# A five-pass graph network on one core: run masks, edge weights and factors put into PSUM, and the relation tiles laid over fewer PSUM banks

## The chip, the cores and the metric

The kernel runs on one core of a Trainium2 chip. Its engines are TensorE (PE, matrix products), VectorE (DVE), ScalarE (ACT), GpSimd (POOL) and SyncE (SP), each with its own instruction stream; they meet through semaphores alone. SBUF is the large on-chip memory, PSUM is a small one of eight banks of 512 fp32 words in each of 128 partitions, which the matrix products write. The metric is the time of one execution on the device in microseconds.

## The reference

Four graph layers run one after the other over 12500 nodes with 16 channels and 400000 edges, which come sorted by target node. Each layer gathers a node's row for each edge, makes a message of it, and sums the messages over the edges of a target; a residual and a normalisation follow.

```python
weights = (relu(edge_attr @ W1 + b1) @ W2 + b2).reshape(-1, 16, 16)   # layer 0
out = segment_sum(einsum('ei,eio->eo', x[src], weights), dst) + x @ root
msg = xw[r] * (dis[r] * ew * dis[c])[:, None]                          # layer 1, twice
msg_tan = einsum('ei,eio->eo', h_tan[src], rel_weight[etype]) + rel_emb[etype]   # layer 2, 230 relations
msg = exp_map_zero(msg_tan, c)
lam = 2.0 / (1.0 - c * jnp.sum(msg * msg, axis=-1) + EPS)
msg = einsum('ei,eio->eo', h_src, W_rel[rel_type]) * e                 # layer 3, 90 relations
x = layernorm(x + layer(x))                                            # after each layer
```

## The kernel before

The work is five passes over all edges, numbered 0 to 4: the edge network (0), two convolutions (1 and 2), and two relation passes (3 and 4). An edge pass takes 125 chunks of 25 tiles of 128 edges, five chunks (slots s = 0 to 4) in each turn of a loop. Between the passes stand short stretches on the nodes, and 100 gathers of the sums at the nodes' ends.

In each chunk GpSimd gathers node rows by indirect DMA, one tile of 128 edges at a time (L637): 25, 14, 14, 21 and 20 tiles of a chunk in passes 0 to 4. The rows of the other tiles ("picks": 11 in a convolution, 4 in pass 3, 5 in pass 4) are made by TensorE: it multiplies a one-hot matrix, built by ScalarE, with the node table cut in four, so that each tile gets 25 candidates for each channel in a PSUM bank (L797 in the convolutions, L855 in the relation passes), and VectorE multiplies them with a selector (`sel`, built at L1254) and sums (L1451 and L1442, or L1292 and L1275).

In the relation passes TensorE also makes each edge's own 16x16 matrix by a one-hot product (L869), 25 tiles in groups, and VectorE multiplies a group with the gathered rows (L1292) and reduces it (L1275). A group is free for TensorE when VectorE's multiplication has read it (semaphore `mats_free`); `mats_wait` looks up in the table `BANKS` the last earlier group whose banks overlap, in the order of the groups, across chunks too, and TensorE waits for that one. In pass 3 the groups of a chunk are one of four picks in banks 4 to 7, six of four tiles that take banks 0 to 3 and 4 to 7 in turn, and one of a single tile in bank 3.

The messages of a chunk go into `acc` with tile as the inner index, and a scan along it (`tensor_tensor_scan`, L1229) forms running sums that start anew where the mask is zero. The mask says for each edge whether its target is that of the edge before; ScalarE spreads it over the channels into SBUF (L889). Before the scan the messages are multiplied: by the edge weight `wgt` in a convolution (L1460), by a factor of the message's norm in pass 3 (L1566), by the edge term in pass 4 (L1650). Pass 3 finishes a chunk within the groups of the next: `finish(it, s, j)` runs after the j-th relation group, and its last piece, the scan, after the sixth.

The order of work is written out by hand; no scheduler moves anything. SP loads the indices of a chunk five chunks ahead, when the sums of the chunk that had the slot are out (`chunks_done`).

```python
            def mats_wait(l, m, it, j):
                n, (b, w) = len(BANKS[l]), BANKS[l][j]
                ago = next(d for d in range(1, n + 1) if BANKS[l][j - d][0] < b + w and b < sum(BANKS[l][j - d]))
                pe.wait_ge(mats_free, it * (S * n) + (m + MFREE + j - ago + 1))
```

Of the kernel before, what the change touches and what calls it, by code (L numbers as in the profile page):

```python
# [38 lines left out]
P = 128  # L39
# [7 lines left out]
] + ["ln_in", "ln_out"] \  # L47
# [3 lines left out]
def build_gnn(nc, x, src, dst, attr, type230, type90, weight, w0a, b0a, w0b, b0b, root0,  # L51
# [20 lines left out]
    NQD = len(QUADS)  # L72
    RH = R2 // 2
# [9 lines left out]
    def first_pick(l):  # L83
# [11 lines left out]
    HALF = [(0, 12), (12, CH - 12)]  # L95
    NCOL = NPK
# [7 lines left out]
        [(slice(CH - PK[l] + t, CH - PK[l] + t + n), n) for t, n in RGRP[l]] + [(slice(t, t + n), n) for t, n in QUADS] for l in (3, 4)]  # L104
    BANKS = [[(2 * (k % 2), 2) for k in range(8)], None, None, [(4, 4)] + [(4 * (i % 2), 4) for i in range(6)] + [(3, 1)],
             [(0, 3), (3, 2), (5, 2), (0, 2), (2, 2), (4, 2), (6, 2), (3, 2), (7, 1)]]
# [51 lines left out]
    with ExitStack() as ctx:  # L158
# [139 lines left out]
        scanned = sem("scanned")  # L298
        term_ready = sem("term_ready")
# [51 lines left out]
        def maskv(s):  # L351
            return mask[:, HOME[s], :].rearrange("p (c t) -> p c t", t=CH + 1)
# [13 lines left out]
        iota_jr = PS[:, 7, 512 - JR:512]  # L366
# [285 lines left out]
        def _(pe):  # L652
# [181 lines left out]
            def relation_pass(l):  # L834
# [10 lines left out]
                with pe.Fori(0, IT) as it:  # L845
                    for s in range(S):
# [11 lines left out]
                        for i, (t0, n) in enumerate(QUADS):  # L858
                            for b, (h0, _) in enumerate(HALF):
                                if t0 == h0:  # L860
                                    pe.wait_ge(oneh_ready, it * (S * 2) + (o0 + 2 * s + b + 1))
# [21 lines left out]
        def _(act):  # L883
            act.wait_ge(ev["w_staged"], 1)
            act.wait_ge(ev["zeroed"], 1)
            def run_mask(l, it, s):

                act.wait_ge(chunks_done, it * S + (NCH * l + s + S - 1))
                act.activation(maskv(s)[:, :, 1:CH + 1], bc_r(same[:, bass.ds(it * (S * CH) + CH * s, CH)], 17),  # L889
                               ACT.Identity).then_inc(masked, 1)  # L890
# [39 lines left out]
            def pick_digits(l):  # L930

                y = PICKED.index(l)
                with act.Fori(0, IT) as it:
                    for s in range(S):
                        act.wait_ge(rows_in[s], it * 16 + (row_base(l) + 16))
                        code = rows_h[:, HOME[s], :]
# [9 lines left out]
                        run_mask(l, it, s)  # L946
# [35 lines left out]
            def one_hots(l, it, s, peeled):  # L982
# [12 lines left out]
                for b, (t0, n) in enumerate(HALF):  # L995
                    if b == 1 and l == 3:
                        if s >= 2:
                            running_out(3, it, s - 2)
                        elif not peeled:
                            running_out(3, it - 1, s + S - 2)  # L1000
                        if s or not peeled:
                            norms(it * S + s)
                    act.wait_ge(mats, it * (S * ng) + (o0 + ng * s - ng + (NPG[l] + 3, ng)[b]))
# [7 lines left out]
                run_mask(l, it, s)  # L1011
                act.drain()

            for s in range(S):
# [4 lines left out]
            running_out(3, IT - 1, S - 2)  # L1019
            norms(NCH)  # L1020
# [3 lines left out]
            root_of("ln_in", na[0:NQ, 3, :], na[0:NQ, 2, :], "ln_out", 3)  # L1024
            for s in range(S):
# [9 lines left out]
        def _(dve):  # L1035
# [186 lines left out]
            def scans(l, it, s):  # L1222

                W = CW[l]
                dve.wait_ge(masked, it * S + (NCH * l + s + 1))
                for c0 in range(0, W, 17 if W == 17 else C):
                    n = min(17 if W == 17 else C, W - c0) * (CH + 1)
                    a = acc[:, HOME[s], c0 * (CH + 1):c0 * (CH + 1) + n]
                    last = dve.tensor_tensor_scan(a, mask[:, HOME[s], 0:n], a, 0.0, ALU.mult, ALU.add)  # L1229
# [205 lines left out]
            def gcn_pass(l):  # L1435
                n = PK[l]
                y = PICKED.index(l)
                then(dve.tensor_copy(iota_jr, iota_f[:, 0:JR]))
# [5 lines left out]
                with dve.Fori(0, IT) as it:  # L1444
                    for s in range(S):
                        chunk_in(l, it, s)
                        nodes_of_bank(l, it, s, iota_jr)
                        for i, (t0, w) in enumerate(GRP):
# [5 lines left out]
                            if i:  # L1454
# [5 lines left out]
                        then(dve.tensor_tensor(accv(s, l)[:, 1:CH + 1, :], gatv(s, l),  # L1460
                                               wgt[:, s, :].unsqueeze(2).to_broadcast([P, CH, C]), ALU.mult))
# [221 lines left out]
```

## Time and profile before

| what | value |
|---|---|
| time, median of 3 runs | 22407.31 us (22362.9 to 22407.92) |
| span of the profiled execution, first to last instruction | 16080.2 us |
| busy share of the span: PE, DVE, ACT, POOL | 77%, 79%, 50%, 74% |
| mean granted TensorE clock | 0.848 |
| time of the passes' gathers on GpSimd, first to last | pass 1 about 2250 us, pass 3 about 3390 us, pass 4 about 3220 us |

The profile gives the span alone; the execution that was profiled has no time of its own beside it. Between the span and the median lie 6327 us that no row of the trace covers. The time of a line is that of its instructions on one engine, and "idle before" is what the engine waited before them and for whom.

### The profile page before, as it was taken

The numbers are of one execution on the slowest core, as the hardware profiler recorded it, in microseconds if no ns is written. First come the engines' busy times: TensorE is split into PE (matmuls) and PEld (weight loads), VectorE is DVE, ScalarE is ACT, GpSimd is POOL, SyncE is SP. The second block draws the span as 40 slices with busy tenths as digits, with TensorE's granted clock in tenths as the row PEclk, the third lists the DMA queues.
The fourth block names the chain that finished last, engine by engine and source line by source line (L and its number), as shares of the span: only waits on it lengthen the run. The fifth ranks groups of instructions, "written<-read, shape, count | busy, mean of one in ns | idle before, by whom it ended". The sixth has DMA issues, their size and how long they took to land.

```text
span 16080.2 us, 197886 instructions
## 1 busy us (share of the span) xinstructions
PE 12414.4 (77%) x62964; PEld 11204.4 (70%) x62964; DVE 12672.3 (79%) x13275; ACT 8008.6 (50%) x6941; POOL 11959.0 (74%) x12266
## 2 busy tenths in 40 slices
PE   6777777777599999599999488888888377777774
PEld 5555555555599998599999377777777376766764
DVE  7777777777577777477777589899989599999996
ACT  1111111111466666466666377777777255555552
POOL 6777777777777777677777677777777577777776
PEclk8888888888799999799999688898888577777776
DMA  1111111111122221122221122222222222222221
GB/s 37 28 27 27 28 28 27 28 28 26 33 40 39 40 39 37 28 40 39 40 39 38 37 48 50 50 51 50 50 47 48 44 61 62 63 60 63 61 62 37
DMA packets 811074, 675.53 MB, mean 42 GB/s; under 512 B 420924, under 2 KB 729500, under 8 KB 810500
## 3 DMA queue, kind: packets, MB, share of 16 engines
q1 hardware_dynamic: 419012, 545.90, 11.4%
q0 software_dynamic: 392000, 128.94, 9.3%
q8 instruction: 23, 0.38, 0.0%
q14 instruction: 39, 0.32, 0.0%
HBM read 507.78 MB, written 166.09 MB: 42 GB/s over the span
## 4 chain that ended last, share of the span: by engine, by line
POOL 57%; issue 20%; DVE 8%; DVEq 8%; PE 6%; DMA 1%; ACT 0%; POOLq 0%; SPq 0%; ACTq 0%
POOL deep L637 54%; DVE big L1292 6%; PE PS L855 5%; DVEq L1040 4%; DVEq L1297 3%; POOL deep L646 3%; DVE sml L1561 0%; DVEq L1232 0%; DVE acc L1229 0%; DMA wgt<-in_edge_weight 0%; DVEq L1286 0%; DVE sml L1553 0%; DVE acc L1566 0%; DVE sml L1554 0%; DVE sml L1558 0%
## 5 line engine op out<-in xcount | busy, mean ns | idle before, releaser
L637 POOL DMA_INDIRECT deep<-table,idx x11750 | 11475.0, 977 | 3824.8 <-issue 3579.0
L797 PE MATMUL PS<-tparts,hot 125*128 125x400 f32 x22000 | 4163.7, 350 | 482.7 <-DVE big L1451 305.4
L797 PEld LDWEIGHTS PS<-tparts,hot 125*128 125x128 f32 x22000 | 4078.7, 192 | 567.4 <-DVE big L1451 387.1
L1292 DVE TENSOR_TENSOR big<-PS,deep 128x768 f32<-128x768 f32 (+4 forms) x2750 | 2984.7, 1085 | 1082.2 <-DMA deep<-table,idx 515.5
L855 PE MATMUL PS<-tparts,rhot 125*128 125x426 f32 (+1 forms) x9000 | 2302.2, 428 | 527.7 <-DVE big L1292 293.8
L855 PEld LDWEIGHTS PS<-tparts,rhot 125*128 125x128 f32 x9000 | 2177.8, 246 | 616.3 <-DVE big L1292 320.7
L944 ACT ACTIVATE hot<-deep,ones_col 128x1536 fp32r<-128x1536 bf16 x1000 | 1447.6, 1472 | 1464.7 <-PE PS L797 1424.8
L754 PE MATMUL PS<-w0b_sb,big 128*128 128x256 f32 x6250 | 1826.1, 437 | 428.4 <-DVE big L1292 390.1
L754 PEld LDWEIGHTS PS<-w0b_sb,big 128*128 128x128 f32 x6250 | 1342.2, 222 | 933.7 <-DVE big L1292 475.0
L869 PE MATMUL PS<-wx,hot 115*128 115x272 f32 x12500 | 1726.1, 293 | 311.1 <-DVE big L1292 311.1
L1275 DVE TENSOR_REDUCE acc<-big 128x64 f32<-128x1024 f32 (+2 forms) x1875 | 1940.6, 1035 | 18.3
L869 PEld LDWEIGHTS PS<-wx,hot 115*128 115x128 f32 x12500 | 1615.0, 188 | 417.5 <-DVE big L1292 397.8
L1451 DVE TENSOR_TENSOR big<-PS,sel 128x1200 f32<-128x1200 f32 x1000 | 1303.8, 1304 | 732.1 <-PE PS L797 644.6
L869 PE MATMUL PS<-w,hot 90*128 90x256 f32 x6250 | 1240.2, 360 | 795.0 <-DVE big L1292 793.8
L904 ACT ACTIVATE big<-PS,b0a_sb 128x512 f32<-128x512 f32 x1000 | 582.8, 597 | 2457.7 <-PE PS L737 2457.7
L869 PEld LDWEIGHTS PS<-w,hot 90*128 90x128 f32 x6250 | 1089.5, 256 | 933.4 <-DVE big L1292 930.5
L1005 ACT ACTIVATE hot<-deep,ones_col 128x3072 fp32r<-128x3072 bf16 (+1 forms) x500 | 1144.7, 2290 | 667.5 <-PE PS L869 667.5
L938 ACT ACTIVATE deep<-wide,negbank 128x1408 bf16<-128x1408 f16 x1000 | 1389.6, 1460 | 78.1 <-DMA wide<-pick_codes 41.9
L1442 DVE TENSOR_REDUCE deep<-big 128x48 f32<-128x1200 f32 x1000 | 1292.1, 1292 | 18.3
L990 ACT ACTIVATE deep<-wide,negrel 128x3200 bf16<-128x3200 bf16 x375 | 1094.5, 2950 | 0.0
L980 ACT COPY msg<-acc 128x425 f32<-128x425 f32 (+1 forms) x250 | 357.5, 1430 | 1423.3 <-DVE acc L1229 1423.3
L1275 DVE TENSOR_REDUCE msg<-big 128x64 f32<-128x1088 f32 x875 | 1011.6, 1156 | 9.2
(281 smaller groups left out, 9713.7 us busy)
## 6 DMA issues: line engine op xcount, KB each, us to landing
wide<-edge_types SPq DMA_DIRECT2D x250, 800.0 KB, 6.1
deep<-table,idx POOLq DMA_INDIRECT x11750, 2.4
wide<-pick_codes SPq DMA_DIRECT2D x250, 352.0 KB, 3.5
running<-msg SPq DMA_DIRECT2D x250, 212.5 KB, 2.1
running<-msg SPq DMA_DIRECT2D x250, 200.0 KB, 2.0
running<-msg SPq DMA_DIRECT2D x125, 400.0 KB, 2.5
wide<-in_edge_attr SPq DMA_DIRECT2D x125, 200.0 KB, 2.5
tabo<-pick_codes SPq DMA_DIRECT2D x125, 160.0 KB, 4.6
```

Of the source, the lines that this page charges most:

```text
L637: pool.indirect_dma_start(g[:, j, 0:GW[l]], None, tab_dram[l][:, :], bass.IndirectOffsetOnAxis(ap=idx[:, s, j:j + 1], axis=0)).then_inc(ga ...
L754: last = pe.matmul(PS[:, b, (u % 2) * CC:(u % 2) * CC + CC], hsb[:, k % 2, u * P:u * P + P], w0b_sb[:, :], start=True, stop=True)
L797: last = pe.matmul(o, poneh[0:NQ, m, c], tparts[0:NQ, k, m * JC:m * JC + JC], start=m == 0 and k == 0, stop=m == BK - 1 and k == 1)
L855: last = pe.matmul(o, rhot[0:NQ, m, c], tparts[0:NQ, k, m * pc:m * pc + pc], start=m == 0 and k == 0, stop=m == BK - 1 and k == 1)
L869: last = pe.matmul(o, oneh[0:K, h, (t0 + u) * P:(t0 + u) * P + P], rhs, start=z == 0, stop=z == len(parts) - 1)
L938: last = act.activation(pdist[:, m, :], code[:, 0:NPK * P], ACT.Abs, bias=negbank[:, m:m + 1])
L944: act.activation(poneh[:, :, c], pdist[:, :, c], ACT.Relu, bias=ones_col[:, 0:1], scale=-1.0).then_inc(poneh_ready, 1)
L1005: act.activation(oneh[:, 0:halves, c], dist[:, 0:halves, c], ACT.Relu, bias=ones_col[:, 0:1], scale=-1.0).then_inc(oneh_ready, 1)
L1275: dve.tensor_reduce(to, products(j), AXX, ALU.add)
L1292: dve.tensor_tensor(products(j), matv(l, j, n), xs, ALU.mult).then_inc(mats_free, 1)
L1442: return dve.tensor_reduce(gatv(s, l)[:, CH - n + t0:CH - n + t0 + w, :], chosen[:, i % 2, 0:w], AXX, ALU.add)
L1451: dve.tensor_tensor(chosen[:, i % 2, 0:w], PS[:, b:b + w, 0:JC].rearrange("p t (c r) -> p t c r", r=JR), sel[:, t0:t0 + w].unsqueeze(2).to ...
```

## The change

In the convolutions slots 0 to 3 keep the mask, a copy of the edge weights and the selector's counting row in PSUM bank 3 or 7 (slot 4 stays in SBUF, its counting row too); ScalarE copies the weights and spreads the mask at the start of its work on a chunk and no longer at its end, and VectorE waits for it at the start of a chunk. In both relation passes mask and factor lie in bank 7, one copy for all slots, so ScalarE writes the mask after the scan of the chunk before; in pass 3 that is in the middle of its work on the next chunk. Bank 7 being taken, the relation tiles of pass 3 go over seven banks: the picks in banks 0 to 3, groups of three and four in banks 4 to 6 and 0 to 3 in turn, a last single tile in bank 3 (nine groups in place of eight). In pass 4 they go over six, with 3 picks in banks 4 to 6 and the rest in pairs of banks 0 to 5.

```diff
+    THREES = [(0, 3), (3, 4), (7, 3), (10, 4), (14, 3), (17, 4), (21, 3), (24, 1)]
+    HALVES_OF = [None, None, None, [(0, 14), (14, CH - 14)], HALF]
...
-    BANKS = [[(2 * (k % 2), 2) for k in range(8)], None, None, [(4, 4)] + [(4 * (i % 2), 4) for i in range(6)] + [(3, 1)],
-             [(0, 3), (3, 2), (5, 2), (0, 2), (2, 2), (4, 2), (6, 2), (3, 2), (7, 1)]]
+    BANKS = [[(2 * (k % 2), 2) for k in range(8)], None, None,
+             [(0, 4)] + [(4, 3) if i % 2 == 0 else (0, 4) for i in range(7)] + [(3, 1)],
+             [(4, 3), (0, 2), (2, 2), (4, 2), (0, 2), (2, 2), (4, 2), (0, 2), (2, 1)]]
...
+        MASK_BANK = [[None] * 5, [3, 7, 3, 7, None], [3, 7, 3, 7, None], [7] * 5, [7] * 5]
+        FLATC = [17, 16, 16, 17, 16]
+        def mask_flat(l, s):
+            n, b = FLATC[l] * (CH + 1), MASK_BANK[l][s]
+            return mask[:, HOME[s], 0:n] if b is None else PS[:, b, 0:n]
+        def chunk_wgt(l, s):
+            b = MASK_BANK[l][s]
+            return wgt[:, s, :] if b is None else PS[:, b, 420:420 + CH]
+        def iota_jr(l, s):
+            b = MASK_BANK[l][s] if l in (1, 2) else None
+            return iota_f[:, 0:JR] if b is None else PS[:, b, 512 - JR:512]
+        fac_ps = PS[:, 7, 460:460 + CH]
...
             def run_mask(l, it, s):
-                act.wait_ge(chunks_done, it * S + (NCH * l + s + S - 1))
-                act.activation(maskv(s)[:, :, 1:CH + 1], bc_r(same[:, bass.ds(it * (S * CH) + CH * s, CH)], 17),
+                if l >= 3:
+                    act.wait_ge(scanned, it * S + (NCH * (l - 3) + s))
+                else:
+                    act.wait_ge(chunks_done, it * S + (NCH * l + s + S - 1))
+                if l in (1, 2) and MASK_BANK[l][s] is not None:
+                    act.sem_inc(act_steps, 1)
+                    act.wait_ge(loaded[s], it * (16 * LOADS[l]) + (ld_base(l) + 16 * LOADS[l]))
+                    act.copy(chunk_wgt(l, s), wgt[:, s, :])
+                act.activation(maskv(l, s)[:, :, 1:CH + 1], bc_r(same[:, bass.ds(it * (S * CH) + CH * s, CH)], FLATC[l]),
                                ACT.Identity).then_inc(masked, 1)
...
                         act.wait_ge(rows_in[s], it * 16 + (row_base(l) + 16))
+                        run_mask(l, it, s)
                         code = rows_h[:, HOME[s], :]
...
-                        run_mask(l, it, s)
                         act.drain()
...
-                    last = dve.tensor_tensor_scan(a, mask[:, HOME[s], 0:n], a, 0.0, ALU.mult, ALU.add)
+                    last = dve.tensor_tensor_scan(a, mask_flat(l, s), a, 0.0, ALU.mult, ALU.add)
...
-                        nodes_of_bank(l, it, s, iota_jr)
+                        dve.wait_ge(masked, it * S + (NCH * l + s + 1))
+                        nodes_of_bank(l, it, s, iota_jr(l, s))
...
-                        then(dve.tensor_tensor(accv(s, l)[:, 1:CH + 1, :], gatv(s, l),
-                                               wgt[:, s, :].unsqueeze(2).to_broadcast([P, CH, C]), ALU.mult))
+                        then(dve.tensor_tensor(accv(s, l)[:, 1:CH + 1, :], gatv(s, l), bc_c(chunk_wgt(l, s)), ALU.mult))
...
-                    then(dve.scalar_tensor_tensor(sml[:, 6, :], sml[:, 5, :], 2.0, sml[:, 4, :], ALU.mult, ALU.mult))
-                    dve.tensor_tensor(accv(s, 3)[:, 1:CH + 1, 0:C], mv, bc_c(sml[:, 6, :]), ALU.mult)
+                    dve.wait_ge(masked, it * S + (NCH * 3 + s + 1))
+                    then(dve.scalar_tensor_tensor(fac_ps, sml[:, 5, :], 2.0, sml[:, 4, :], ALU.mult, ALU.mult))
+                    dve.tensor_tensor(accv(s, 3)[:, 1:CH + 1, 0:C], mv, bc_c(fac_ps), ALU.mult)
...
                         if i == 1:
-                            dve.tensor_tensor(sml[:, 1, :], term[:, s, :], gatv(s, 4)[:, :, C], ALU.add)
+                            dve.wait_ge(masked, it * S + (NCH * 4 + s + 1))
+                            dve.tensor_tensor(fac_ps, term[:, s, :], gatv(s, 4)[:, :, C], ALU.add)
```

VectorE at the end of a chunk of pass 3, before the change. The rows go from the multiplication of the last, single tile (272 elements) to that of the next chunk's picks (1600 elements); `big` holds the products, `msg` the sums, and the scan is printed as `SCALAR_TENSOR_TENSOR acc<-mask,acc`.

```order
L1292 TENSOR_TENSOR big<-PS,deep 128x272
L1275 TENSOR_REDUCE msg<-big 128x4x16
L1229 SCALAR_TENSOR_TENSOR acc<-mask,acc 128x442
L1233 COPY acc<-acc 128x17
L1275 TENSOR_REDUCE msg<-big 128x16
L1576 TENSOR_TENSOR big<-msg 128x400
L1577 TENSOR_REDUCE sml<-big 128x25
L1578 TENSOR_SCALAR sml<-sml 128x25
L1254 ISA
L1254 TENSOR_TENSOR sel<-iota_f,rsel 128x100
L1286 REGISTER_ALU
L1292 TENSOR_TENSOR big<-PS,sel 128x1600
```

The same place after the change, from the multiplication of the last group but one (three tiles, 816 elements).

```order
L1331 TENSOR_TENSOR big<-PS,deep 128x816
L1314 TENSOR_REDUCE msg<-big 128x4x16
L1268 SCALAR_TENSOR_TENSOR acc<-PS,acc 128x442
L1272 COPY acc<-acc 128x17
L1325 REGISTER_ALU
L1331 TENSOR_TENSOR big<-PS,deep 128x272
L1314 TENSOR_REDUCE msg<-big 128x3x16
L1314 TENSOR_REDUCE msg<-big 128x16
L1620 TENSOR_TENSOR big<-msg 128x400
L1621 TENSOR_REDUCE sml<-big 128x25
L1622 TENSOR_SCALAR sml<-sml 128x25
L1293 ISA
```

With nine groups the sixth relation group is no longer the last but one of the chunk, so the scan, its copy and the reduction of four tiles now stand ahead of the last tile's multiplication and no longer behind it.

ScalarE in a convolution before the change, one chunk: four distances for the one-hots (L938), four groups of one-hots (L944), each of which waits for TensorE, and the mask of the chunk.

```order
L938 ACTIVATE deep<-wide,negbank 128x1408 x4
L942 REGISTER_ALU
L944 ACTIVATE hot<-deep,ones_col 128x4x384
L942 REGISTER_ALU
L944 ACTIVATE hot<-deep,ones_col 128x4x384
L942 REGISTER_ALU
L944 ACTIVATE hot<-deep,ones_col 128x4x384
L942 REGISTER_ALU
L944 ACTIVATE hot<-deep,ones_col 128x4x256
L888 REGISTER_ALU
L889 ISA
L889 ACTIVATE mask<-same 128x17x25
```

The same after the change, for a slot whose mask lies in PSUM.

```order
L917 COPY PS<-wgt 128x25
L918 ISA
L918 ACTIVATE PS<-same 128x16x25
L969 ACTIVATE deep<-wide,negbank 128x1408 x4
L973 REGISTER_ALU
L975 ACTIVATE hot<-deep,ones_col 128x4x384
L973 REGISTER_ALU
L975 ACTIVATE hot<-deep,ones_col 128x4x384
L973 REGISTER_ALU
L975 ACTIVATE hot<-deep,ones_col 128x4x384
L973 REGISTER_ALU
L975 ACTIVATE hot<-deep,ones_col 128x4x256
```

The mask, with its wait for the chunk before the last, has moved ahead of the distances, and the copy of the weights is new.

## Rows read from the trace of the kernel before

**Rows 1.** The page's first line.

```profile
span 16080.2 us, 197886 instructions
```

**Rows 2.** GpSimd's gathers by line in pass 1, pass 3 and pass 4.

```profile
L637 POOL DMA_INDIRECT deep<-table,idx x1750 | 1714.8, 980 | 564.9 <-issue 533.0 <-DMA wgt<-in_edge_weight 31.9
...
L637 POOL DMA_INDIRECT deep<-table,idx x2625 | 2590.6, 987 | 848.3 <-issue 799.4 <-DMA idx<-in_src 48.9
...
L637 POOL DMA_INDIRECT deep<-table,idx x2500 | 2455.8, 982 | 832.8 <-issue 761.6 <-DMA term<-edge_term 71.1
```

**Rows 3.** Timeline of pass 1: start us, us, engine, line, operation, idle before.

```profile
5004.58 5.56 ACT L938 ACTIVATE deep<-wide,negbank 128x1408 bf16<-128x1408 f16 x4
5004.92 0.95 POOL L637 DMA_INDIRECT deep<-table,idx  x1 [0.30 <-issue]
...
5007.21 0.95 DVE L1460 TENSOR_TENSOR acc<-deep,wgt 128x400 f32<-128x400 f32 x1 [0.95 <-DMA deep<-table,idx]
5007.43 1.40 POOL L637 DMA_INDIRECT deep<-table,idx  x1 [0.30 <-issue]
...
5009.53 0.92 DVE L1237 COPY msg<-acc 128x400 f32<-128x400 f32 x1
5010.29 3.05 ACT L944 ACTIVATE hot<-deep,ones_col 128x1536 fp32r<-128x1536 bf16 x2
...
5020.41 0.99 DVE L1451 TENSOR_TENSOR big<-PS,sel 128x800 f32<-128x800 f32 x1 [0.19 <-PE PS L797]
...
5021.47 0.54 ACT L889 ACTIVATE mask<-same 128x425 bf16 x1
```

**Rows 4.** Waits of pass 3, window 9200 to 12400: total us, times, longest.

```profile
DVE big L1292 <- PE PS L855: 80.4, 94, 1.0
```

**Rows 5.** VectorE by line and form in pass 3, window 9200 to 12400.

```profile
L1292 DVE TENSOR_TENSOR big<-PS,deep 128x1088 f32<-128x1088 f32 x708 | 913.3, 1290 | 96.1 <-issue 30.7
L1275 DVE TENSOR_REDUCE msg<-big 128x64 f32<-128x1088 f32 x708 | 903.5, 1276 | 0.0
...
L1292 DVE TENSOR_TENSOR big<-PS,sel 128x1600 f32<-128x1600 f32 x118 | 215.4, 1825 | 85.2 <-PE PS L855 80.4 <-issue 4.8
...
L1292 DVE TENSOR_TENSOR big<-PS,deep 128x272 f32<-128x272 f32 x118 | 52.1, 442 | 17.2
```

**Rows 6.** Timeline of one chunk of pass 3.

```profile
11000.97 0.57 DVE L1576 TENSOR_TENSOR big<-msg 128x400 f32<-128x400 f32 x1
...
11003.15 1.83 DVE L1292 TENSOR_TENSOR big<-PS,sel 128x1600 f32<-128x1600 f32 x1 [0.20 <-issue]
...
11021.59 7.64 PE L855 MATMUL PS<-tparts,rhot 125*128 125x400 f32 x32 [2.44 <-DVE big L1292]
...
11024.08 0.44 DVE L1292 TENSOR_TENSOR big<-PS,deep 128x272 f32<-128x272 f32 x1
...
11025.63 1.07 DVE L1229 TENSOR_TENSOR_SCAN acc<-mask,acc 128x442 f32<-128x442 bf16 x1
...
11027.05 0.44 DVE L1275 TENSOR_REDUCE msg<-big 128x16 f32<-128x272 f32 x1
...
11029.75 1.82 DVE L1292 TENSOR_TENSOR big<-PS,sel 128x1600 f32<-128x1600 f32 x1 [0.20 <-issue]
```

**Rows 7.** Chain of work that ended last, within pass 3: start us, us, what.

```profile
11182.09 1.30 DVE big L1292
11183.44 8.87 PE PS L855 x32
11192.34 1.83 DVE big L1292
```

**Rows 8.** Busy us by engine in one stretch: PE, PEld, DVE, ACT, POOL, then granted clock.

```profile
11021.60:11029.20 7.60, 7.60 (x33) 7.58 (x34) 6.83 (x12) 3.14 (x4) 5.83 (x6) 0.78 0.13 20
```

**Rows 9.** Timeline of VectorE in pass 4: the copy that ends a chunk.

```profile
13956.61 0.20 DVE L1233 COPY acc<-acc 128x32 f32<-128x32 f32 x1
...
13981.84 0.20 DVE L1233 COPY acc<-acc 128x32 f32<-128x32 f32 x1
```

More of the change, by code:

```diff
@@ L857, in relation_pass @@
                             last.then_inc(mats, 1)
-                        for i, (t0, n) in enumerate(QUADS):
-                            for b, (h0, _) in enumerate(HALF):
+                        for i, (t0, n) in enumerate(THREES if l == 3 else QUADS):
+                            for b, (h0, _) in enumerate(HALVES_OF[l]):
                                 if t0 == h0:
@@ L994, in one_hots @@
                 act.activation(rhot[:, :, 0:w], rdist[:, :, 0:w], ACT.Relu, bias=ones_col[:, 0:1], scale=-1.0).then_inc(poneh_ready, 1)
-                for b, (t0, n) in enumerate(HALF):
+                for b, (t0, n) in enumerate(HALVES_OF[l]):
                     if b == 1 and l == 3:
@@ L1000, in one_hots @@
                             running_out(3, it - 1, s + S - 2)
+                        if s:
+                            run_mask(3, it, s - 1)
+                        elif not peeled:
+                            run_mask(3, it - 1, S - 1)
                         if s or not peeled:
                             norms(it * S + s)
-                    act.wait_ge(mats, it * (S * ng) + (o0 + ng * s - ng + (NPG[l] + 3, ng)[b]))
+                    act.wait_ge(mats, it * (S * ng) + (o0 + ng * s - ng + (NPG[l] + (4 if l == 3 else 3), ng)[b]))
                     c = slice(t0 * P, t0 * P + n * P)
@@ L1019, in _ @@
             running_out(3, IT - 1, S - 2)
+            run_mask(3, IT - 1, S - 1)
             norms(NCH)
@@ L1224, in scans @@
                 W = CW[l]
[L1225 to L1228, printed above, removed]
-                    last = dve.tensor_tensor_scan(a, mask[:, HOME[s], 0:n], a, 0.0, ALU.mult, ALU.add)
+                if l == 0:
+                    dve.wait_ge(masked, it * S + (NCH * l + s + 1))
+                n = FLATC[l] * (CH + 1)
+                for c0 in range(0, W * (CH + 1), n):
+                    a = acc[:, HOME[s], c0:c0 + n]
+                    last = dve.tensor_tensor_scan(a, mask_flat(l, s), a, 0.0, ALU.mult, ALU.add)
                 if l >= 3:
@@ L1437, in gcn_pass @@
                 y = PICKED.index(l)
-                then(dve.tensor_copy(iota_jr, iota_f[:, 0:JR]))
+                for s in range(2):
+                    dve.memset(maskv(l, s)[:, :, 0], 0.0)
+                    dve.tensor_copy(iota_jr(l, s), iota_f[:, 0:JR])
+                dve.drain()
+                dve.sem_inc(ev["banks_set"], 1)
                 def pick_sum(s, i):
@@ L1584, in _ @@
                     hyper_chunk(it, s, lambda j, s=s: finish(it - (s == 0), (s - 1) % S, j))
-            for j in range(NQD):
+            for j in range(len(THREES)):
                 finish(IT - 1, S - 1, j)
@@ L1637, in _ @@
             table_parts(4)
+            dve.memset(maskv(4, 0)[:, :, 0], 0.0)
+            dve.drain()
+            dve.sem_inc(ev["banks_set"], 1)
             with dve.Fori(0, IT) as it:
```

26 lines of the change are left out of this document (17 added, 9 removed).

## The prediction, made before the change was run

> **What bounds the kernel now.** I read the gathers of GpSimd by line first, then a timeline of a chunk in each kind of pass, then the waits and the chain of pass 3, and for single costs the groups by form. The span is 16080.2 us [rows 1], the median 22407.31; the 6327 us between them lie in no row. I count everything against the span and take the rest as unchanged, so a difference of the span is taken as the same difference of the median. That is a choice, and one rival below turns on it.
>
> *Convolutions.* A gather takes 0.95 us and 0.30 of issue, so 14 of them take 17.5 us a chunk. The rows of pass 1 give (1714.8 + 533.0) / 125 = 17.98 us; pass 2 has the same mean [rows 2, 3]. GpSimd waits for nothing else within the pass, and VectorE sits idle 0.95 us for the gather ahead of L1460: GpSimd sets the pace. The missing 0.48 us are single gathers that take longer: the one at 5007.43 takes 1.40 us, and under it runs L1460, whose two inputs both lie in SBUF [rows 3]. The scan, with mask and sums in SBUF, comes next and has two SBUF inputs as well. The change takes one of the two out of SBUF.
>
> *Pass 3.* Here GpSimd is not the bound, though its gathers are as continuous: 27.12 us a chunk, where 21 undisturbed ones would take 26.25 [rows 2, 3]. VectorE never waits for a gather in this stretch, but in 94 of 118 chunks for the pick product L855 (80.4 us) [rows 4]. The chain shows the ring: VectorE's multiplication of the sixth relation group ends at 11183.39, the picks of the next chunk start 0.05 later (their banks 4 to 7 are free then), take 8.87, and VectorE multiplies them 0.03 after that [rows 7]. In the chunk of [rows 6] the picks take 7.64 and VectorE comes 0.5 us later than they do. So product and VectorE are level now: while the picks run, VectorE still has the single tile, the scan and the norms to do.
>
> *Pass 4.* GpSimd's rate is (2455.8 + 761.6) / 125 = 25.74 us a chunk, 25.0 undisturbed [rows 2, 3]; VectorE needs 25.23 where it waits for no gather [rows 9].
>
> **The change, part by part.** *Stretched gathers in the convolutions.* In four of five slots neither the weighting nor the scan has two SBUF inputs any more: 0.48 x 4/5 x 125 = 48 us a pass. Slot 4 keeps both and now builds its selector from SBUF too; that can stretch a gather of its own, and I take 3 us for it. So -45 us for each convolution. Bounds: 0, if other instructions fall onto the gathers instead, and -60.
>
> *Mask at the start of ScalarE's work.* ScalarE now waits for the end of the chunk before the last ahead of its distances. In [rows 3] that end is at 5010.45 (L1237). From there: copy of the weights, bounded above by the mask's 0.54 since it has 25 columns in place of 425, the mask 0.54, the distances 5.56, the first half of the 3.05 for two one-hot groups, together 8.2, to 5018.6. TensorE is free for that group at 5020.41, when VectorE gets the last picks of the chunk before. It is hidden with 1.8 us to spare, and costs nothing up to there. Queued behind it on ScalarE are the one-hots for TensorE, and VectorE waits for those products.
>
> *Pass 3: nine groups in seven banks.* This is the term that decides. The picks now go to banks 0 to 3, and the single tile of the chunk before sits in bank 3. By the rule in `mats_wait` the picks wait for the group just before them, so TensorE may start on the picks only when VectorE has multiplied the last tile. Before it was the last but one, and between the two lay the work that hid the product. What VectorE does from its first multiplication to the end of the single tile's was 11003.15 to 11024.52, 21.37 us, and from there to the next chunk's first 5.23 [rows 6]. Added to the first part:
> - one multiplication more: 1088 and 272 elements take 1.290 and 0.442, so 0.283 a tile and 0.16 fixed [rows 5], with a gap of 0.1: 0.26;
> - one reduction more ahead of it, and 21 tiles in place of 20: 0.14 fixed, 0.28 for the tile, 0.1 gap: 0.52;
> - the scan with its copy, which moves ahead of the last tile: 11025.63 to 11027.05, 1.42 [rows 6].
>
> That makes 23.57. The second part falls to 5.23 - 1.42 - 0.28 = 3.53. Without a wait the chunk would be 27.1 us, as now. But the picks start at the end of the first part, and 3.5 us cover less than half of them: the chunk is 23.57 + 0.05 + picks + 0.03.
>
> The duration of the picks is open, since TensorE stands idle before them longer than now: 2.44 us in [rows 6], and about 6 us after the change (the fifth reduction, the factor, two multiplications, a reduction and the scan lie between its single tile and the start). The granted clock over the 7.6 us of [rows 8] is 0.78, so the product would take 7.6 x 0.78 = 5.9 at 2.4 GHz throughout and 11.9 at 1.2 throughout. The observed ones are 7.64 and 8.87. I take 7.6: an idle time is before them in both cases, and the clock came back within the product. Then the chunk takes 31.25, 4.13 more than 27.12, and over 124 chunks +512 us. Bounds: picks of 5.9 give 29.55 and +301; picks of 11.9 give 35.55 and +1045. GpSimd, freed from stretching there, gains nothing: it waits for slots.
>
> *Pass 3, mask.* ScalarE writes it in the middle of the next chunk, behind the same wait for the scan that its copy of the sums had; 0.54 us, and VectorE asks for it five groups later. Nothing.
>
> *Pass 4.* No stretching by weighting or scans: GpSimd could run at 25.0, VectorE needs 25.23, so 0.5 x 125 = -60 us. Its picks still start after the fifth of seven relation groups, as now in effect. Bounds 0 and -92.
>
> *PSUM as an operand.* A multiplication with one PSUM input takes 0.16 + 0.283 for each 272 elements, 0.58 for 400 by [rows 5]; L1576 with two SBUF inputs takes 0.57 for 400 [rows 6]. I count no difference. The Trainium skill ("VectorE: DVE Perf Modes", section "The TRN2 errata") has a fixed 120 cycles for PSUM sources against 58 for SBUF sources, about 65 ns at its 0.96 GHz. By it the two touched instructions of pass 3 and three of pass 4 would cost an estimated 40 us more, and the time would be 22,810; these rows do not bear it out.
>
> **Sum.** -45 - 45 + 512 - 60 = +362 us on the span: 16,442 in place of 16,080, and **22,770 us** on the median.
>
> **Rivals.** *The gathers set the pace where the time is taken.* If the 6327 us outside the span are not a fixed cost but slower gathers in the timed executions, they are 0.52 us on each of 12250 (94 a chunk in 125 chunks, and 500 at the ends), and 21 gathers take 37 us a chunk: more than the 31.25 of the new ring, which is then hidden. It decides from 31.25 / 21 = 1.49 us a gather on. Left is the stretching saved, 45 + 45 + 60 and at most 0.87 x 125 = 109 in pass 3, half of it for L1576 staying as it is: -205, about 22,200 us, faster. For it speaks only the unexplained time; against it that 1.25 us is what the profile shows from end to end.
>
> *The wait is not there.* If the picks could still start after the last group but one, as now in effect, the 512 would shrink to the extra group's fixed costs, at most 0.5 x 124 = 62 us: -88, about 22,320. Only a misreading of the table could bring it.
>
> *The clock stays down.* TensorE is idle for longer stretches all through pass 3; if the picks run at 1.2 GHz throughout, +1045 replaces 512: 23,300. Against it: in [rows 8] the level recovers within the product.
>
> *ScalarE late in the convolutions.* The spare 1.8 us is partly eaten by a faster GpSimd (0.4). If the chain is 2.4 us longer than summed, each chunk is 1 us longer, 250 in all, and the 90 gained are lost: 23,110.
>
> **How the numbers follow.** The forecast gets 0.70; its own range is 22,620 to 23,020 (picks of 6.7 to 8.9, gains between 60 and 200). The clock gets 0.08, ScalarE 0.07, the gathers 0.11, the missing wait 0.04. The low end of the range is the forecast's low end with 40 us for what the sum leaves out, 22,580; the high end takes in the clock, 23,300; outside lie the two faster cases, 0.15, and tails. A run of this kernel tells 0.2% (45 us) from no change, as the three runs lie 45 us apart. Faster by more than that: 0.14; within: 0.02; slower: 0.84.
>
> **What would show it.** In pass 3 each pick product starts within 0.1 us of the end of a 272-element multiplication, VectorE waits 4 us or more there in every chunk, and the chunk takes about 31 us. In passes 1 and 2 the mean gather falls from 980 towards 955 ns and VectorE still waits for gathers; in pass 4 gathers are rarely stretched and VectorE no longer waits for them. Wrong would be: a chunk of 27 us in pass 3; a product of 6 or of 11 us; a wait for ScalarE's one-hots by TensorE in the convolutions; or a span that grows while the time does not.

## The result, and the profile after the change

| | median us | runs | range |
|---|---|---|---|
| before | 22407.61 | 4 | 22362.9 to 22444.36 |
| after | 23023.12 | 4 | 22986.38 to 23038.78 |

After takes 1.0275 times as long as before (95% interval 1.0258 to 1.0292): 615 us slower. Forecast were 22,770 us and a range of 22,580 to 23,300, so the sign and the range held and the value was 253 us too low.

The profiled execution of after took 22986.38 us, and its span is 22984.6:

```profile
span 22984.6 us, 198878 instructions
```

So 1.8 us lie around the program. The 6327 us that the prediction left outside the span are no such thing. The first profile of before [rows 1] shows an execution that ran in 16,080 us; all timed executions of the same program lie between 22,320 and 22,464 us and are that much longer inside. Numbers of after must therefore be held against a second profile of before, which experiment e0 below took: span 22387.7 us. In the two traces the passes, from the first gather to the last scan, last:

| pass | first profile of before | second profile of before (e0) | after | after less e0 |
|---|---|---|---|---|
| 0 | 3965.5 | 5801.9 | 5794.9 | -7.0 |
| 1 | 2251.2 | 2996.7 | 2964.4 | -32.3 |
| 2 | 2250.7 | 2987.9 | 2971.6 | -16.3 |
| 3 | 3433.3 | 5600.3 | 6231.5 | +631.2 |
| 4 | 3241.4 | 4060.4 | 4085.5 | +25.1 |

They sum to +601 of the 597 us between the spans. Pass 3 carries the loss and a little more.

GpSimd's gathers by line in passes 1, 3 and 4 of after, the rows that answer to [rows 2]:

```profile
L659 POOL DMA_INDIRECT deep<-table,idx x1750 | 1657.9, 947 | 1286.3 <-DMA wgt<-in_edge_weight 764.2 <-issue 522.1
...
L659 POOL DMA_INDIRECT deep<-table,idx x2625 | 2486.0, 947 | 3702.6 <-DMA idx<-in_src 2939.1 <-issue 763.5
...
L659 POOL DMA_INDIRECT deep<-table,idx x2500 | 2365.1, 946 | 1712.1 <-DMA term<-edge_term 986.7 <-issue 725.4
```

A gather takes 947 ns and none is stretched, but GpSimd now waits 764, 2939 and 987 us for loads of the next chunk's indices, weights or terms, which start when a slot is free: in none of them is it at work from end to end, as the prediction had it. Pass 3 takes (2486.0 + 3702.6) / 125 = 49.5 us a chunk.

VectorE by line and form in pass 3 of after, window 12900 to 17900, which answers to [rows 4, 5]:

```profile
L1331 DVE TENSOR_TENSOR big<-PS,deep 128x816 f32<-128x816 f32 x404 | 406.3, 1006 | 751.1 <-remote 690.2 <-PE PS L891 30.3
...
L1331 DVE TENSOR_TENSOR big<-PS,deep 128x1088 f32<-128x1088 f32 x303 | 391.4, 1292 | 1178.0 <-remote 1059.7 <-issue 96.2 <-PE PS L891 1.2
...
L1331 DVE TENSOR_TENSOR big<-PS,sel 128x1600 f32<-128x1600 f32 x101 | 184.3, 1825 | 479.6 <-issue 316.5 <-PE PS L877 163.2
...
L1268 DVE TENSOR_TENSOR_SCAN acc<-PS,acc 128x442 f32<-128x442 f32 x101 | 107.8, 1067 | 0.0
L1610 DVE TENSOR_TENSOR acc<-msg,PS 128x400 f32<-128x400 f32 x101 | 91.0, 901 | 7.6
...
L1331 DVE TENSOR_TENSOR big<-PS,deep 128x272 f32<-128x272 f32 x101 | 44.6, 442 | 14.8
```

Before the picks' multiplication (128x1600) VectorE waits 479.6 / 101 = 4.75 us in each chunk. Here the wait stands mostly under "issue", a reason that the profile doesn't name; the timeline of one chunk, which answers to [rows 6], shows what it is:

```profile
14007.29 1.07 DVE L1268 TENSOR_TENSOR_SCAN acc<-PS,acc 128x442 f32<-128x442 f32 x1
...
14008.78 0.44 DVE L1331 TENSOR_TENSOR big<-PS,deep 128x272 f32<-128x272 f32 x1
...
14009.27 7.50 PE L877 MATMUL PS<-tparts,rhot 125*128 125x400 f32 x32 [5.42 <-DVE big L1331]
...
14012.39 0.26 DVE L1293 TENSOR_TENSOR sel<-iota_f,rsel 128x100 f32<-128x100 f32 x1 [0.20 <-issue]
...
14013.21 0.95 POOL L659 DMA_INDIRECT deep<-table,idx  x1 [23.50 <-DMA idx<-in_src]
...
14016.81 1.82 DVE L1331 TENSOR_TENSOR big<-PS,sel 128x1600 f32<-128x1600 f32 x1 [4.16 <-issue]
...
14018.69 2.27 PE L891 MATMUL PS<-wx,hot 115*128 115x272 f32 x16 [0.41 <-issue]
...
14021.52 1.78 PE L891 MATMUL PS<-wx,hot 115*128 115x272 f32 x12 [0.55 <-DVE big L1331]
...
14028.11 1.29 DVE L1331 TENSOR_TENSOR big<-PS,deep 128x1088 f32<-128x1088 f32 x1 [6.65 <-remote]
...
14038.23 0.95 POOL L659 DMA_INDIRECT deep<-table,idx  x1 [0.30 <-issue]
14042.83 1.01 DVE L1331 TENSOR_TENSOR big<-PS,deep 128x816 f32<-128x816 f32 x1 [12.52 <-remote]
...
14045.67 1.29 DVE L1331 TENSOR_TENSOR big<-PS,deep 128x1088 f32<-128x1088 f32 x1 [0.15 <-issue]
...
14056.80 1.07 DVE L1268 TENSOR_TENSOR_SCAN acc<-PS,acc 128x442 f32<-128x442 f32 x1
```

The single tile's multiplication ends at 14009.22, the picks start 0.05 us later, TensorE having been idle 5.42 us for just that, they take 7.50 us, and VectorE goes on 0.04 us after them. That is the ring of the prediction. The rest of the rows shows what it did not know: 6.65 and 12.52 us of waiting for relation products within one chunk, with "remote" as the releaser (no engine of this trace), the second wait ending 3.65 us after the last of the 21 gathers that run beside it (14038.23 + 0.95). In the same stretch of the chain that ended last:

```profile
14008.78 0.44 DVE big L1331
...
14012.81 4.01 issue
14016.81 1.82 DVE big L1331
...
14021.60 6.49 another core or an unknown queue
14028.11 1.29 DVE big L1331
...
14030.42 12.39 another core or an unknown queue
```

For [rows 8]: over the picks of this chunk the granted clock is 0.79 of 2.4 GHz, where it was 0.78 before (busy us by engine, then the clock):

```profile
14009.30:14016.80 7.50, 7.50 (x34) 7.47 (x35) 2.86 (x6) 6.09 (x7) 2.84 (x3) 0.79 0.60 152
```

For [rows 9], two chunk ends of pass 4 of after lie 34.1 us apart (the mean of the pass is 31.9), where the first profile of before had 25.23:

```profile
20529.59 0.20 DVE L1272 COPY acc<-acc 128x32 f32<-128x32 f32 x1
20563.69 0.20 DVE L1272 COPY acc<-acc 128x32 f32<-128x32 f32 x1
```

### The profile page after: what moved, and what is told of

The parts are those of the page before. It is cut to its first block, busy times and chain, and to the rows that moved or that the text cites. A ratio compares the mean times of both kernels' runs of the same rounds, so it can differ in the third digit from the quotient of the medians.

```text
span 22984.6 us, 198878 instructions
## 1 busy us (share of the span) xinstructions
PE 13976.1 (61%) x62964; PEld 12375.4 (54%) x62964; DVE 12653.1 (55%) x13533; ACT 8010.3 (35%) x7141; POOL 11606.4 (50%) x12266
## 4 chain that ended last, share of the span: by engine, by line
PE 25%; another core or an unknown queue 23%; DVE 21%; DVEq 15%; issue 15%; POOL 1%; ACT 0%; DMA 0%; SPq 0%; ACTq 0%; POOLq 0%
PE PS L819 15%; DVE big L1331 10%; DVEq L1336 9%; PE PS L877 5%; DVEq L1078 3%; DVE big L1495 2%; DVE acc L1268 1%; PE PS L776 1%; DVE wide L1382 1%; POOL deep L668 1%; DVE Y L1383 1%; PE PS L759 1%; DVEq L1500 1%; PE PS L891 1%
## 5 line engine op out<-in xcount | busy, mean ns | idle before, releaser
L659 POOL DMA_INDIRECT deep<-table,idx x11750 | 11122.5, 947 | 10804.5 <-issue 3449.0
L1331 DVE TENSOR_TENSOR big<-PS,deep 128x768 f32<-128x768 f32 (+5 forms) x2875 | 3004.1, 1045 | 5451.7 <-remote 4668.0
L819 PE MATMUL PS<-tparts,hot 125*128 125x400 f32 x22000 | 4646.2, 372 | 1435.6 <-issue 986.0
L819 PEld LDWEIGHTS PS<-tparts,hot 125*128 125x128 f32 x22000 | 4431.3, 208 | 1650.2 <-issue 1316.1
L891 PE MATMUL PS<-wx,hot 115*128 115x272 f32 x12500 | 2243.3, 343 | 2263.7 <-issue 1141.5
L877 PE MATMUL PS<-tparts,rhot 125*128 125x426 f32 (+1 forms) x9000 | 2471.9, 441 | 1715.3 <-DVE big L1331 824.5
L891 PEld LDWEIGHTS PS<-wx,hot 115*128 115x128 f32 x12500 | 2055.9, 236 | 2446.3 <-DVE big L1331 1257.8
L1039 ACT ACTIVATE hot<-deep,ones_col 128x3584 fp32r<-128x3584 bf16 (+1 forms) x500 | 1146.5, 2293 | 3548.4 <-remote 2439.3
L759 PE MATMUL PS<-atT,tabo 128*128 128x512 f32 x2000 | 1136.0, 658 | 305.6 <-issue 305.4
L1331 DVE TENSOR_TENSOR big<-PS,sel 128x850 f32<-128x850 f32 (+1 forms) x375 | 544.3, 1452 | 1246.3 <-remote 575.2
```

The source lines that it names most:

```text
L659: pool.indirect_dma_start(g[:, j, 0:GW[l]], None, tab_dram[l][:, :], bass.IndirectOffsetOnAxis(ap=idx[:, s, j:j + 1], axis=0)).then_inc(ga ...
L759: pe.matmul(PS[:, 4 + k % 2, 0:n], w0blk[:, k, :], atT[:, 0:n], start=True, stop=True).then_inc(h_psum, 1)
L819: last = pe.matmul(o, poneh[0:NQ, m, c], tparts[0:NQ, k, m * JC:m * JC + JC], start=m == 0 and k == 0, stop=m == BK - 1 and k == 1)
L877: last = pe.matmul(o, rhot[0:NQ, m, c], tparts[0:NQ, k, m * pc:m * pc + pc], start=m == 0 and k == 0, stop=m == BK - 1 and k == 1)
L891: last = pe.matmul(o, oneh[0:K, h, (t0 + u) * P:(t0 + u) * P + P], rhs, start=z == 0, stop=z == len(parts) - 1)
L1331: dve.tensor_tensor(products(j), matv(l, j, n), xs, ALU.mult).then_inc(mats_free, 1)
```

## The experiments

"A chunk" below is the mean distance of chunks in the pass in question, by the ends of the gathers, from the tenth chunk on.

**e0: the kernel before once more, for a second profile.** No edit.

> The kernel before, unchanged, for a second profile. In the profile of after, time and span differ by 1.8 us, and even the untouched pass 0 takes 45.7 us a chunk where the first profile of before has 31.6. If the executions that are timed are slower inside the program (theory A), this profile shows a span of about 22,400 us, pass 0 at about 45 us a chunk, and TensorE's instructions starting about 0.7 us apart for stretches of tens of us, as in the profile of after. If the 6327 us lie around the program (theory B, the choice that the prediction made), the span is again near 16,080 us.

Theory A held. 22389.51 us, and the page's first line:

```profile
span 22387.7 us, 197886 instructions
```

GpSimd's gathers in passes 1, 3 and 4 and VectorE's multiplications in pass 3 (window 12900 to 17400) of this profile:

```profile
L637 POOL DMA_INDIRECT deep<-table,idx x1750 | 1668.7, 954 | 1302.0 <-DMA wgt<-in_edge_weight 752.1 <-issue 544.4 <-DMA idx<-in_src 5.4
...
L637 POOL DMA_INDIRECT deep<-table,idx x2625 | 2485.3, 947 | 3088.4 <-DMA idx<-in_src 2325.2 <-issue 763.3
...
L637 POOL DMA_INDIRECT deep<-table,idx x2500 | 2435.7, 974 | 1617.7 <-DMA term<-edge_term 890.2 <-issue 727.6
...
L1292 DVE TENSOR_TENSOR big<-PS,deep 128x1088 f32<-128x1088 f32 x607 | 783.0, 1290 | 1877.9 <-remote 1615.9 <-issue 142.0 <-PE PS L869 98.8
L1292 DVE TENSOR_TENSOR big<-PS,sel 128x1600 f32<-128x1600 f32 x101 | 184.3, 1825 | 37.3 <-PE PS L855 29.7 <-issue 7.6
```

Each instruction costs what it cost in the first profile (1290 and 1825 ns, [rows 5]), but VectorE waits 1877.9 / 101 = 18.6 us a chunk for relation products, most of them "remote", where [rows 5] had 96.1 us in 118 chunks. GpSimd waits 752 us in pass 1 already before the change. TensorE's starts at multiples of about 0.70 us do occur, in some 340 stretches and 2,700 us of this trace (stretches with four or more such steps, to 0.03 us; two in the first profile), but none of them lies in pass 3; there the two traces differ mainly by these waits. Before the picks' multiplication VectorE waits 37.3 / 101 = 0.37 us.

**e1: the convolutions alone.** Passes 3 and 4 have their old order, banks and operands; the main lines of the edit, against after:

```diff
-        MASK_BANK = [[None] * 5, [3, 7, 3, 7, None], [3, 7, 3, 7, None], [7] * 5, [7] * 5]
+        MASK_BANK = [[None] * 5, [3, 7, 3, 7, None], [3, 7, 3, 7, None], [None] * 5, [None] * 5]
...
-             [(0, 4)] + [(4, 3) if i % 2 == 0 else (0, 4) for i in range(7)] + [(3, 1)],
-             [(4, 3), (0, 2), (2, 2), (4, 2), (0, 2), (2, 2), (4, 2), (0, 2), (2, 1)]]
+             [(4, 4)] + [(4 * (i % 2), 4) for i in range(6)] + [(3, 1)],
+             [(0, 3), (3, 2), (5, 2), (0, 2), (2, 2), (4, 2), (6, 2), (3, 2), (7, 1)]]
```

> Only the convolutions are changed (passes 1 and 2: mask, weights and counting row in PSUM, mask early on ScalarE); passes 3 and 4 are those of the kernel before. The prediction's term is -45 us for each convolution, so about 22,315 us. If in the timed executions something other than the gathers sets the pace of the convolutions (TensorE's picks), the term is 0 and the time 22,405; if the early mask holds up ScalarE, 22,500 or more.

22378.09 us, 0.9982 of before (0.9972 to 0.9993): 43 us faster, half of the term. Of the versions that compute everything it is the fastest of the study.

**e2: the convolutions and pass 4.** Of the lines above only those of pass 3 are taken back.

> The change in the convolutions and in pass 4; pass 3 is that of the kernel before. The prediction's terms are -90 and -60: 22,260 us. If pass 3 carries the whole loss, nothing else being moved, the time is 23,023 less the loss of pass 3: 22,400 or below. If the loss is spread over the passes (TensorE slower everywhere), 22,600 to 22,800.

22420.08 us, 1.0001 (0.9992 to 1.0011). So pass 4 costs 42 us on top of e1 where 60 us of gain stood in the sum, and pass 3 the remaining 23,023 - 22,420 = 603 us (617 when each of the two is held against the runs of the kernel before that stand beside it, 22,407.61 and 22,421.57). The profiles agree: pass 4 lasts 4062.1 us in e1 and 4090.5 in e2; its chunk is 31.45 to 31.70 us in the five profiles up to e7 that have the old layout, and 31.87 to 32.01 in the four that have the new one.

**e3: the last tile of pass 3 in another bank.**

```diff
-             [(0, 4)] + [(4, 3) if i % 2 == 0 else (0, 4) for i in range(7)] + [(3, 1)],
+             [(0, 4)] + [(4, 3) if i % 2 == 0 else (0, 4) for i in range(7)] + [(6, 1)],
```

> The whole change, but the last single tile of pass 3 goes to bank 6 in place of bank 3, so that the picks of the next chunk wait for the multiplication before the last one, as in the kernel before; the single tile then waits for that same multiplication. Ring theory (the picks' wait for the last tile is the loss): pass 3 gets back 2 to 3 us of the 4 a chunk, 250 to 370 us, so 22,650 to 22,770. If the loss comes of the nine groups in seven banks as such, or of TensorE's slow starts whatever it waits for: 23,020 as before, within 60.

22676.18 us, 1.0118 (1.0101 to 1.0135): 347 us come back by one number in the table, as the ring has it. The chunk is 46.65 us, and VectorE's wait before the picks' multiplication, in 101 chunks of this kernel (after: 479.6), is

```profile
L1331 DVE TENSOR_TENSOR big<-PS,sel 128x1600 f32<-128x1600 f32 x101 | 184.3, 1825 | 202.2 <-PE PS L877 194.5 <-issue 7.6
```

2.0 us each, down by 2.75, as the chunk is by 2.82.

**e4 and e5: half of the pick products, before and after.** In pass 3 the picks leave out the low-order half of the table.

```diff
-                                    for k in range(2):
+                                    for k in range(1 if l == 3 else 2):
```

> The kernel before, but the picks of pass 3 leave out the low-order half of the table: 16 products in place of 32. Ring theory: in the kernel before the picks lie beside work of VectorE that is as long as they are, so pass 3 stays within 1 us of its 44.4 us a chunk (125 us in all). If the picks are on the path before as well, the chunk falls by about 4 us, to 40.4.

> The kernel after with the same omission, 16 products in place of 32 in pass 3. Ring theory: here the picks begin only after the last tile and VectorE waits 4 us for them in each chunk, so the chunk falls by 3.5 to 4.5 us, from 49.4 to about 45.4, nearly the kernel before's. If the loss comes of the nine groups or of TensorE's slow stretches instead, it stays at 48.5 or more.

Each is one run. e4: 22375.34 us beside 22352.14 of the kernel before on the same chip; the chunk is 44.39 us, as in e0 (44.38), though the product falls from 7.95 to 4.86 us in the mean. e5: 22642.35 us, 381 below after; the product falls from 8.14 to 5.20 us, by 2.94, and the chunk from 49.47 to 46.59, by 2.88. So a shorter product is worth nothing before the change and shortens the chunk after it, by as much as the product itself; what that equality is worth is taken up with the ring below. The 3.5 to 4.5 us expected were too many since half the products take more than half the time.

**e6 and e7: half of the relation products, half of the gathers, in the kernel before.** Both ask what the 18.6 us of waiting come from. e6 leaves out the low-order half of the relation table, e7 gathers every second tile.

```diff
-                parts = [(h, k) for h in range(halves) for k in range(2)]
+                parts = [(h, k) for h in range(halves) for k in range(1 if l == 3 else 2)]
```

```diff
         cols = [j for j in range(CH) if not first_pick(l) <= j < first_pick(l) + PK[l]]
+        if l == 3:
+            cols = cols[::2]
```

> The kernel before, but pass 3 leaves out the low-order half of the relation products: 50 in place of 100 a chunk. VectorE waits 18 us a chunk for these products in the second profile of before and under 1 us in the first. If those waits grow with the number of TensorE's instructions (theory N), the chunk falls from 44.4 to about 38 us. If they come with the gathers that run beside (theory G) or by the chunk, it stays at 43 to 45.

> The kernel before, but pass 3 gathers only every second of its 21 tiles (11, about half; the others keep old rows). Theory G, the waits come with the gathers running beside: they fall by about half and the chunk from 44.4 to about 36 us. Theory N, they grow with TensorE's instructions: 44 as before.

e6: 21823.29 us, chunk 39.63; e7: 20898.99 us, chunk 32.93. VectorE's waits before a relation group in e7, 97 chunks:

```profile
L1294 DVE TENSOR_TENSOR big<-PS,deep 128x1088 f32<-128x1088 f32 x584 | 753.4, 1290 | 696.6 <-remote 578.6 <-PE PS L871 57.1 <-issue 29.7
```

7.2 us a chunk in place of 18.6. Neither theory is alone right, since e6 falls too, but the gathers weigh most: 11.45 us of chunk for 10 gathers.

**e8: all orders, tiles and banks of after, with every operand in SBUF.**

```diff
-        MASK_BANK = [[None] * 5, [3, 7, 3, 7, None], [3, 7, 3, 7, None], [7] * 5, [7] * 5]
+        MASK_BANK = [[None] * 5] * 5
...
-                    dve.tensor_tensor(accv(s, 3)[:, 1:CH + 1, 0:C], mv, bc_c(fac_ps), ALU.mult)
+                    dve.tensor_tensor(accv(s, 3)[:, 1:CH + 1, 0:C], mv, bc_c(sml[:, 6, :]), ALU.mult)
...
```

> The kernel after in every order, tile size and bank, but masks, weights, counting rows and factors stay in SBUF (ScalarE's copy of the weights falls away with them). Ring theory: pass 3 and pass 4 lose by the layout of the tiles alone, so pass 3 stays at 49.4 us a chunk and pass 4 at 31.9, and the whole near 23,020 to 23,070 us. If the operands in PSUM themselves cost time in pass 3 or 4, those chunks fall (the skill's fixed cost of PSUM sources would give about 0.2 us each). In the convolutions it tells where the 0.2 us a chunk came from: 23.5 us again if from the operands, 23.3 if from ScalarE's order.

23003.13 us, 1.0282 (1.0266 to 1.0298), as after. Chunks: pass 3 49.51 us, pass 4 31.90. VectorE's scan and its factor multiplication in pass 3 of e8, window 12900 to 17900:

```profile
L1268 DVE TENSOR_TENSOR_SCAN acc<-mask,acc 128x442 f32<-128x442 bf16 x101 | 108.0, 1069 | 0.0
...
L1609 DVE TENSOR_TENSOR acc<-msg,sml 128x400 f32<-128x400 f32 x101 | 91.4, 905 | 7.5
```

1069 and 905 ns with operands in SBUF, 1067 and 901 with them in PSUM: the place of the operands is worth nothing there (the factor is fp32 in both; the mask is bf16 in SBUF and fp32 in PSUM), and the layout of the tiles, with the order of work that goes with it, does the whole loss of passes 3 and 4. The two convolutions together last 5955 us in e8. With the old convolutions they last 5959 to 6020 us in five profiles (e0, e4, e6, e7, e10), with the changed ones 5933 to 5963 in six (after, e1, e2, e3, e5, e9). So e8 lies within the changed ones and just below the old ones: the gain of e1 seems to be there without PSUM, but one profile doesn't settle it, and its two passes take 23.25 and 23.43 us a chunk, one near each of the two values that the expectation set apart.

**e9: an attempt at a better pass 3.** e1, with the single tile of pass 3 as the first relation group (the one-hots are then handed over after 13 tiles and no longer after 12). The line of the banks, against e1:

```diff
-             [(4, 4)] + [(4 * (i % 2), 4) for i in range(6)] + [(3, 1)],
+             [(4, 4), (0, 1)] + [(4 * ((i + 1) % 2), 4) for i in range(6)],
```

> The kernel with only the convolutions changed, and in pass 3 (mask in SBUF, eight banks) the single tile is the first relation group in place of the last, so that the last group behind the picks' start has four tiles and covers 1.7 us more. VectorE waits 0.4 us a chunk before the picks' multiplication in the second profile of before, so at most 46 us are to be had: about 22,330. Against it: the short group now stands where TensorE must make the next four tiles in the time of a single one, and where products come late that loses up to 1 us a chunk: 22,500.

22714.26 us, 1.0149 (1.0136 to 1.0163): a miss, beyond what was feared. In 101 chunks VectorE now waits 19.9 us in all for the picks, but 2213.2 us for the relation groups:

```profile
L1325 DVE TENSOR_TENSOR big<-PS,deep 128x1088 f32<-128x1088 f32 x606 | 782.7, 1292 | 2213.2 <-remote 1799.8 <-PE PS L891 220.0 <-issue 152.0
```

21.9 us a chunk against 18.6. With the short group first, VectorE has nine tiles behind it and not twelve when it comes to the fourth relation group, where most of the waiting is in both kernels (15.0 us a chunk here, 13.0 in e0).

**e10: a quarter of the gathers.** As e7 with `cols[::4]`.

> The kernel before, but pass 3 gathers 6 of its 21 tiles (every fourth; the others keep old rows). With 21 gathers VectorE waits 19 us a chunk for relation products, with 11 it waits about 7. If the waits go with the gathers (theory G), they fall below 4 us here and the chunk to 28 to 30 us, near the 26.4 that VectorE's work fills without them. If something else holds TensorE back and the half-gather run only shifted it, the chunk stays above 32.

20276.99 us, chunk 27.45 us. VectorE's waits before a relation group in 94 chunks:

```profile
L1294 DVE TENSOR_TENSOR big<-PS,deep 128x1088 f32<-128x1088 f32 x570 | 735.1, 1290 | 158.8 <-PE PS L871 78.8 <-issue 29.1 <-remote 10.6
```

1.7 us a chunk, and "remote" has all but gone. With 21, 11 and 6 gathers the waits are 18.6, 7.2 and 1.7 us, as theory G has it.

## Why the prediction was right in sign and short in size

**The ring of pass 3: right in its steps, near in price by luck in part.** Each step shows as it was put: in every chunk from the tenth on the picks start 0.05 to 0.06 us after the single tile's multiplication, and VectorE waits 4.75 us where it waited 0.37. (Counted from one, the scan stands behind the seventh relation group, the last before the change and the last but one after it.) An earlier start (e3) and a shorter product (e5) each bring back 2.8 to 2.9 us a chunk. The term was mis-sized: +512 in the sum, +603 or +617 by e2 and after, +631 by the two profiles; in a chunk 5.09 us in place of 4.13. What was sized too small is the 7.6 us for the picks, the shorter of two that were looked at. After the change they last 8.14 us in the mean, and in the 125 chunks of the prediction's own profile 8.58, which puts 23.57 + 0.05 + 8.58 + 0.03 = 32.23 us and +634 into its sum. The waits before all relation groups hardly differ: (751.1 + 1178.0 + 14.8) / 101 = 19.2 us against (1877.9 + 14.8) / 101 = 18.7. The clock rival (picks of 11.9 us) did not come about.

The chunk itself is not the sum of VectorE's work and one wait that the prediction adds up: that gave 31.25 us, and 49.5 are measured. In the longer executions it is a round through the gathers. In the rows of after above the scan ends at 14008.36, the first gather of the next batch starts at 14013.21, the last ends at 14039.18, VectorE's last long wait ends at 14042.83, and the next scan starts at 14056.80. In the means, us a chunk (long is a wait before a relation group of over 1.5 us):

| | scan to first gather | the batch of gathers | last gather to the end of the last long wait | from there to the end of the scan | chunk |
|---|---|---|---|---|---|
| e0 | 4.8 | 25.9 | 2.9 | 10.7 | 44.4 |
| after | 4.8 | 26.0 | 3.5 | 15.3 | 49.5 |
| e3 | 4.8 | 25.9 | 3.5 | 12.4 | 46.7 |
| e5 | 4.8 | 25.9 | 3.7 | 12.2 | 46.6 |
| e6 | 4.8 | 25.9 | 2.5 | 6.5 | 39.7 |
| e7, 11 gathers | 4.8 | 13.5 | 2.1 | 12.5 | 32.9 |
| e9 | 4.8 | 25.9 | 3.3 | 13.4 | 47.5 |

With 21 gathers the kernels differ mostly in the last part: in how much VectorE still has to do when its last long wait ends. That is most often at the third relation group in after, at the fourth in e3, e5 and e9, at the fourth or fifth in e0 and at the sixth in e6. The picks' wait itself lies mostly beside the batch (14012.81 to 14016.81 in the rows, the batch from 14013.21 on); by these rows late picks cost time in that VectorE has fewer groups behind it when the last long wait begins. From the third to the fourth relation group are 2.84 us (14042.83 to 14045.67), about what e3 and e5 bring back, so it may be chance that e5's chunk fell by just the length of the product: no run tells the two readings apart. That the price of the ring came out near in a chunk that is made up in another way was not foreseen.

**The gathers: wrong, by the first choice of the prediction.** The 45 us for each convolution and the 60 us for pass 4 rest on GpSimd setting the pace, which it does in the first profile of before alone. The step that failed is "I count everything against the span and take the rest as unchanged". The unexplained 6327 us were doubted in one rival only, and with the wrong content: gathers of 1.77 us, that is GpSimd even more the bound. Measured is the opposite, gathers of 0.95 us and a GpSimd that waits in every pass. A gather less stretched then saves little or nothing: 954 to 947 ns in pass 1, while its waits stay (1302.0 and 1286.3 us), and 974 to 946 ns in pass 4, 70 us of gathers in all, in a pass that became 25 us longer. In pass 3 the batch is part of the round, as the table shows, but its gathers take 947 ns on either side of the change.

**Convolutions: -43 in place of -90.** What is left of the gain comes, as far as e8 tells, not from PSUM but from the mask's place at the start of ScalarE's work and VectorE's wait for it, a step that was costed at nothing. With the spread that e8's paragraph gives, this is suggested and not settled. ScalarE late in the convolutions, the rival, is excluded by the sign.

**Pass 4: +42 in place of -60.** Here, too, GpSimd is not the bound, and the layout over six banks costs 0.3 us a chunk with the operands in SBUF as in PSUM (e8). By the two profiles VectorE's waits before the four-tile groups grow from 221.4 / 101 to 287.5 / 100 us a chunk, and those before the single tile shrink by 0.3. Which group's shorter lead does it was not tried.

**PSUM as an operand: right at nothing.** e8 and after differ by 20 us of 23,000, with the intervals of their ratios overlapping. The larger fixed cost of PSUM sources that the Trainium skill states ("VectorE: DVE Perf Modes", section "The TRN2 errata"), an estimated 40 us here, does not show: the scan and the factor multiplication take the same with either place, to 4 ns.

The predicted value was thus low by 105 us in pass 3 (617 against 512), 47 in the convolutions and 102 in pass 4, which makes up the 253 us; the errors do not cancel each other.

## What to carry to other kernels

Before a profile is costed, hold its span against the timed runs of the same program; where they differ by a quarter, ask first for the profile of a timed execution, since the bound itself may be another one. When a buffer is moved to free a bank, go through the table of who waits for whom: one number (bank 3 or 6 for a single tile) decided whether a product of 8 us lay beside other work, and it can be found on paper. Cover gained at one end of a ring can be lead lost at the other (e9), so a new order is costed at all its waits. And before a wait is priced, follow the round that it stands in: what runs beside the wait, here a batch of gathers, decides what it costs.

## What the runs showed of the hardware that was not expected

- The same program ran once in 16,080 us and otherwise in 22,320 to 22,464. In the longer executions VectorE waits for relation products that TensorE's records show as done: in the rows of after above, a product of 16 matmuls begins at 14018.69 and takes 2.27 us, and the multiplication that needs it starts at 14028.11. The trace has the update of the semaphore that VectorE waits for (`mats`) at 14028.09, 7.1 us after the record's end, and that for the next group, recorded to 14023.30, at 14042.81, 19.5 us after; so VectorE waits here for the signal of the product and not for gathered rows or a store. Whether the record is early or the signal late no run tells.
- These waits go with the gathers that run beside them (18.6, 7.2, 1.7 us a chunk for 21, 11, 6 gathers) and fall also with half the relation products (1379.5 / 101 = 13.7 us in e6). The last of them mostly ends a fixed time after the batch's last gather: 3.57 to 3.74 us in nine of ten chunks of after, 3.4 to 3.8 in two of three of e0, 2.05 to 2.28 in all of e7. Why, no run tells. The gathers alone are not the cause: in the first profile of before they ran without a pause, with under 1 us of such waits a chunk. What set that execution apart stays open.
